# One attention stage of a fused two-layer model: values first, one tiled run per step, input normalised by GpSimd

## The reference

```python
q = (x @ Wq + bq).reshape(B, S, H, Dh).transpose(0, 2, 1, 3)   # x = layernorm(h), H = 12, Dh = 16
k = (x @ Wk + bk).reshape(B, S, H, Dh).transpose(0, 2, 1, 3)
v = (x @ Wv + bv).reshape(B, S, H, Dh).transpose(0, 2, 1, 3)
scores = jnp.einsum('bhqd,bhkd->bhqk', q, k) / SCALE
attn = jax.nn.softmax(scores, axis=-1)
out = jnp.einsum('bhqk,bhkd->bhqd', attn, v)
out = out.transpose(0, 2, 1, 3).reshape(B, S, D)
return out @ Wo + bo                                            # h = h + this
```

## Time and profile before

| what | us |
|---|---|
| median of three runs | 1070.24 (1067.24 to 1072.44) |
| the profiled execution | 1065.48 |
| its span | 1063.7 |
| PE busy | 801.3 (75%) |
| VectorE busy | 580.3 (55%) |
| ScalarE busy | 427.6 (40%) |
| GpSimd busy | 302.2 (28%) |

### The profile page before, as it was taken

The page is one execution under the profiler, slowest core; times in us unless marked ns, Lnnn a source line. Parts: engine busy times, 40 slices in busy tenths (PEclk is TensorE's granted clock), DMA queues, the critical chain, the costliest instruction groups (busy, mean ns, idle before and its releaser), DMA issues. The chain is left out here.

```text
span 1063.7 us, 22703 instructions
## 1 busy us (share of the span) xinstructions
PE 801.3 (75%) x7528; PEld 664.2 (62%) x7529; DVE 580.3 (55%) x1434; ACT 427.6 (40%) x1054; POOL 302.2 (28%) x293
## 2 busy tenths in 40 slices
PE   2489999998779814444455698895349999999993
PEld 2367777776679502222234476674249999999993
DVE  1757777776545101111116488886975666555562
ACT  4355666565543300000000267653524444444441
POOL 1300001000023000000000157761575555555552
PEclk7699999997555766666687699997558999999997
DMA  9391000000000398998960830002611333332331
GB/s 269 105 428 57 1 0 0 0 0 1 1 1 2 113 347 352 381 349 325 337 231 6 318 132 1 0 0 59 161 50 32 53 52 52 47 51 50 52 52 19
DMA packets 37999, 119.33 MB, mean 112 GB/s; under 512 B 7538, under 2 KB 28436, under 8 KB 33588
## 3 DMA queue, kind: packets, MB, share of 16 engines
q1 hardware_dynamic: 24980, 104.30, 26.9%
q0 software_dynamic: 10848, 12.67, 7.4%
q10 hardware_dynamic: 2112, 1.57, 0.9%
HBM read 105.77 MB, written 11.14 MB: 110 GB/s over the span
## 5 line engine op out<-in xcount | busy, mean ns | idle before, releaser
L1012 PE MATMUL psum<-flat,m_yT 64*32 64x384 f32 x624 | 45.8, 648 | 105.2 <-issue 103.9
L1629 POOL DMA_INDIRECT out_h<-x_ys,idx x55 | 87.5, 1591 | 98.9 <-ACT x_ys L1654 80.5
L1753 PE MATMUL psum<-w_pairs,x_h_hi 128*128 x330 | 101.7, 370 | 1.1 <-DVE x_h_lo L1681 1.1
L1012 PEld LDWEIGHTS psum<-flat,m_yT 64*32 64x32 f32 x624 | 16.9, 138 | 128.7 <-issue 128.4
L969 DVE COPY f_hid<-psum 128x384 f32<-128x384 f32 x16 | 8.9, 558 | 147.4 <-PE psum L1012 147.4
L1755 PE MATMUL psum<-w_pairs,x_h_lo 128*128 x330 | 82.7, 251 | 0.0
L1681 DVE TENSOR_TENSOR x_h_lo<-psum,x_h_hi 128x384 fp32r<-128x384 f32 x110 | 56.3, 553 | 38.7 <-ACT x_h_hi L1650 38.6
L1205 POOL MEMSET b_ones<- 96x96 f32 x1 | 0.2, 176 | 242.2 <-POOLq L130 242.2
L461 POOL TENSOR_TENSOR flat<-flat,a_bo 96x192 f32 (+1 forms) x32 | 18.7, 586 | 174.5 <-DVE a_xn L520 174.5
L534 DVE TENSOR_REDUCE a_mx<-psum 96x12 f32<-96x1152 f32 x32 | 43.3, 1353 | 44.0 <-PE psum L610 44.0
L1654 ACT ACTIVATE x_ys<-x_ys,cw 128x192 f32<-128x192 f32 x55 | 25.1, 456 | 102.0 <-DVE x_ys L1692 102.0
(11 more groups left out here) (271 smaller groups left out, 2293.8 us busy)
## 6 DMA issues: line engine op xcount, KB each, us to landing
flat<-in_slot_w SPq DMA_DIRECT2D x27, 2304.0 KB, 21.4
ring_last<-in_slot_w SPq DMA_DIRECT2D x5, 2304.0 KB, 28.9
flat<-in_moe_w SPq DMA_DIRECT2D x1, 10752.0 KB, 29.3
flat<-in_x_patches SPq DMA_DIRECT2D x4, 1536.0 KB, 16.2
out_h<-flat SPq DMA_DIRECT2D x1, 2304.0 KB, 12.2
xtab<-flat SPq DMA_DIRECT2D x4, 576.0 KB, 4.0
m_y<-in_fc_b SPq DMA_DIRECT2D x1, 1536.0 KB, 19.5
m_y<-f_y2g ACTq DMA_DIRECT2D x16, 96.0 KB
```

What stands on the lines that cost most here:

```text
L1012: mm = pe.matmul(b_h[n][r][B * c:B * (c + 1), :], g.yT[rows, k, SC * gr + c, :], w1[c // 2][rows, c % 2, k, n * N2:(n + 1) * N2], start=(k ...
L1629: pool.indirect_dma_start(out=A["out"][:, :], out_offset=bass.IndirectOffsetOnAxis(ap=g.idx[:, i:i + 1], axis=0), in_=ys[:, i % 2, :], in_ ...
L1753: pe.matmul(b_y[u % 2], h_hi[:, k, :], g.w_pairs[:, :, k, bass.ds(e, 1), :].rearrange("p two a d -> p two (a d)"), start=(k == 0), stop=False)
```

## The change

The edits, all within `attention0`:

- PE's order becomes values (lag 4, was 3; all three rounds in a row), scores, transpose of x, eight turns, output, q projection, last four turns, k and v projection.
- `project` is cut in two: q with its own semaphores, then k and v. The k part waits until ScalarE has copied q, since both lie in one PSUM bank, and the v part until x of the next batch has been copied out of bank 0.
- ScalarE's order becomes x copy, two copies of turned rounds, q copy, third copy, k copies, v copy, exponent (lag 2, was 3).
- VectorE's order becomes division, maximum, residual (lag 4, was 5), subtraction; the normalisation goes to GpSimd, ahead of the bias.

```diff
+            def norm_input(b, i):
+                reused(pool, s_xTp, b, 2)
+                pool.tensor_scalar(xn[:, i % 2, :].unsqueeze(1), g.h[:, bass.ds(b, 1), :], g.rstd[:, bass.ds(b, 1)],
+                                   g.nmr[:, bass.ds(b, 1)], ALU.mult, ALU.add).then_inc(s_xn, 1)
...
-            steps(pool, B, [(add_bias, 0)])
+            few_steps(B, [(norm_input, 0), (add_bias, 0)], UNROLL)
...
+            def q_copy(b, i):
+                item(act, s_qp, b)
                 reused(act, s_sc, b, 2)
-                act.activation(qT[:, i % 2, :, :], bank_qk[:, 0:2, :], ACT.Copy)
+                act.activation(qT[:, i % 2, :, :], bank_q[:, :, :], ACT.Copy).then_inc(s_qs, 1)
...
-            steps(act, B, [(exponent, 3), (qk_copy, 1), (v_copy, 1), (p_copy_first, 3), (x_copy, 0),
-                           (p_copy_last, 3)])
+            steps(act, B, [(x_copy, 0), (p_copy_first, 3), (q_copy, 1), (p_copy_last, 3), (k_copy, 1), (v_copy, 1),
+                           (exponent, 2)])
...
-            few_steps(B, [(divide, 4), (residual, 5), (norm_input, 0), (maximum, 2), (subtract, 2)], UNROLL)
+            few_steps(B, [(divide, 4), (maximum, 2), (residual, 4), (subtract, 2)], UNROLL)
...
+            def project_kv(b, i):
+                item(pe, s_qs, b)
+                for m in range(2, 4):
+                    mm = project(bank_k, i % 2, m)
+                mm.then_inc(s_kp, 1)
+
+                pe.wait_ge(s_xTs, min(b + 2, B) if isinstance(b, int) else b + 2)
...
+            def values(b, i):
                 item(pe, s_vs, b)
-
-                reused(pe, s_res, b, 2)
+                item(pe, s_pTs, b, NG)
+
+                reused(pe, s_res, b, 1)
                 reused(pe, s_oTs, b, 1)
-                values(b, i, 0)
-                turn(b, i, 2)
-                values(b, i, 1)
-                values(b, i, 2).then_inc(s_oTp, 1)
+                for r in range(NG):
...
-            steps(pe, B, [(project, 1), (turn_first, 3), (score, 2), (transpose_x, 0), (attend, 3), (output, 4)])
+            steps(pe, B, [(values, 4), (score, 2), (transpose_x, 0), (turn_first, 3), (output, 4), (project_q, 1), (turn_last, 3),
+                          (project_kv, 1)])
```

More of the change, by code:

```diff
@@ L429, in attention0 @@
         s_set, s_vset = sem("set"), sem("vset")
-        s_xn, s_bo, s_xTp, s_xTs, s_qkp, s_vp, s_qks, s_vs = (
-            sem(n) for n in ("xn", "bo", "xTp", "xTs", "qkp", "vp", "qks", "vs"))
+        s_xn, s_bo, s_xTp, s_xTs, s_qp, s_kp, s_vp, s_qs, s_ks, s_vs = (
+            sem(n) for n in ("xn", "bo", "xTp", "xTs", "qp", "kp", "vp", "qs", "ks", "vs"))
         s_sc, s_mx, s_sub, s_exp, s_sum = (sem(n) for n in ("sc", "mx", "sub", "exp", "sum"))
@@ L438, in attention0 @@
         bank_x = g.ps[:, 0, :]
-        bank_qk = g.ps[0:HALF, 1, 0:4 * T].rearrange("p (m t) -> p m t", t=T)
+        bank_q = g.ps[0:HALF, 1, 0:2 * T].rearrange("p (m t) -> p m t", t=T)
+        bank_k = g.ps[0:HALF, 1, 2 * T:4 * T].rearrange("p (m t) -> p m t", t=T)
         bank_oT = g.ps[:, 2, 0:NG * T].rearrange("p (r t) -> p r t", t=T)
@@ L478, in x_copy, with k_copy @@
                                bank_x[0:HALF, 0:2 * T].rearrange("p (k t) -> p k t", k=2), ACT.Copy).then_inc(s_xTs, 1)
-            def qk_copy(b, i):
-                item(act, s_qkp, b)
+            def q_copy(b, i):
+                item(act, s_qp, b)
                 reused(act, s_sc, b, 2)
-                act.activation(qT[:, i % 2, :, :], bank_qk[:, 0:2, :], ACT.Copy)
+                act.activation(qT[:, i % 2, :, :], bank_q[:, :, :], ACT.Copy).then_inc(s_qs, 1)
+            def k_copy(b, i):
+                item(act, s_kp, b)
+                reused(act, s_sc, b, 2)
                 for par in range(2):
-                    ins = act.activation(kT[:, i % 2, :, par, :], bank_qk[:, 2:4, :], ACT.Copy, scale=hmask[:, par:par + 1])
-                ins.then_inc(s_qks, 1)
+                    ins = act.activation(kT[:, i % 2, :, par, :], bank_k[:, :, :], ACT.Copy, scale=hmask[:, par:par + 1])
+                ins.then_inc(s_ks, 1)
             def v_copy(b, i):
@@ L496, in exponent, with p_copy @@
                 act.activation(p[:, i % 2, :, :], p[:, i % 2, :, :], ACT.Exp, scale=DH ** -0.5).then_inc(s_exp, 1)
[L498 to L503, removed]
+            def p_copy(b, r):
+                act.wait_ge(s_pTp, b * NG + r + 1)
+                reused(act, s_oTp, b, 1)
+                act.activation(pT[:, r, :, :], bank_pT[r].rearrange("p (h t) -> p h t", t=T), ACT.Copy).then_inc(s_pTs, 1)
             def p_copy_first(b, i):
-                p_copy(b, (0, 1))
+                p_copy(b, 0)
+                p_copy(b, 1)
             def p_copy_last(b, i):
-                p_copy(b, (2,))
-            steps(act, B, [(exponent, 3), (qk_copy, 1), (v_copy, 1), (p_copy_first, 3), (x_copy, 0),
-                           (p_copy_last, 3)])
+                p_copy(b, 2)
+            steps(act, B, [(x_copy, 0), (p_copy_first, 3), (q_copy, 1), (p_copy_last, 3), (k_copy, 1), (v_copy, 1),
+                           (exponent, 2)])
             layernorm_scale(None, act, g, s_ln)
@@ L516, in _ @@
         def _(v):
[L518 to L521, removed]
             def residual(b, i):
@@ L584, in transpose_x @@
                 item(pe, s_xn, b)
-                reused(pe, s_vs, b, 1)
+                reused(pe, s_vs, b, 2)
+                reused(pe, s_xTs, b, 1)
                 for hf in range(2):
@@ L589, in transpose_x, with project, project_q @@
                 mm.then_inc(s_xTp, 1)
-            def project(b, i):
-                item(pe, s_xTs, b)
-                reused(pe, s_qks, b, 1)
-                k = i % 2
[L595 to L600, removed]
+            def project(bank, xk, m):
+                pe.matmul(bank[:, m % 2, :], wqk[0:HALF, 0, m * HALF:(m + 1) * HALF], xT[0:HALF, xk, 0, :],
+                          start=True, stop=False)
+                return pe.matmul(bank[:, m % 2, :], wqk[:, 1, m * HALF:(m + 1) * HALF], xT[:, xk, 1, :],
+                                 start=False, stop=True)
+            def project_q(b, i):
+                item(pe, s_xTs, b)
+                reused(pe, s_ks, b, 1)
+                for m in range(2):
+                    mm = project(bank_q, i % 2, m)
+                mm.then_inc(s_qp, 1)
+            def project_kv(b, i):
[4 more added lines that the diff above has]
+                pe.wait_ge(s_xTs, min(b + 2, B) if isinstance(b, int) else b + 2)
+                k = i % 2
                 pe.matmul(bank_x[0:T, 2 * T:2 * T + D], xT[0:HALF, k, 0, :], wv[0:HALF, 0, :], start=True, stop=False)
@@ L604, in score @@
             def score(b, i):
-                item(pe, s_qks, b)
+                item(pe, s_ks, b)
                 reused(pe, s_sub, b, 1)
@@ L618, in turn @@
                 mm.then_inc(s_pTp, 1)
[L620 to L625, removed]
             def turn_first(b, i):
@@ L631, in turn_first, with turn_last @@
                 turn(b, i, 1)
-            def attend(b, i):
+            def turn_last(b, i):
+                pe.wait_ge(s_pTs, b * NG + 1)
+                turn(b, i, 2)
+            def values(b, i):
                 item(pe, s_vs, b)
-                reused(pe, s_res, b, 2)
+                item(pe, s_pTs, b, NG)
+                reused(pe, s_res, b, 1)
                 reused(pe, s_oTs, b, 1)
-                values(b, i, 0)
-                turn(b, i, 2)
-                values(b, i, 1)
-                values(b, i, 2).then_inc(s_oTp, 1)
+                for r in range(NG):
+                    for j in range(HG):
+                        mm = pe.matmul(bank_oT[HPAD * j:HPAD * (j + 1), r, :], vv[:, i, head_at(r, j), :], pT[:, r, j, :],
+                                       start=True, stop=True, tile_position=(0, HPAD * j))
+                mm.then_inc(s_oTp, 1)
             def output(b, i):
```

## The result

The changed kernel takes 1052.36 us (median of four runs, 1051.24 to 1054.57) against 1069.05 for the kernel before (four runs, 1067.24 to 1072.44). The ratio is 0.985, its 95% interval 0.981 to 0.989: faster by 1.5%. The forecast was 1046.4 and the range 1036 to 1062. The direction and the mechanism in the steps held; the gain, 16.7 us, is 0.7 of the 23.8 forecast, and the parts are further off than the sum. The kernel before ran again beside the experiments, in three groups with medians of 1067.87, 1065.80 and 1067.67 us; against those the gain is 13.4 to 15.5. The profiled execution took 1051.24 (span 1049.3); there the stage, from the first slot product on PE to the last statistics, fell from 221.0 to 207.7 us.

What follows compares the result with a forecast made beforehand. PE was taken to set the pace: 28 steps shortened by 0.68 us give 19.0, fill 1.5 and drain 3.3, together 23.8 us off the 1070.24 median: 1046.4 us, range 1036 to 1062.

Steps and rivals of the forecast that it cites:

- PE sets the pace of the steps: First attention's 28 steps: PE's order alone takes each from 6.35 to 5.67 us, 19.0 us in all.
- The normalisation's move: Normalisation on GpSimd instead of VectorE: 0.6 us taken there, fits in the step, costs nothing; VectorE's 0.3 is off the path.
- The new wait for the q copy: PE at the k projection: release 0.58 us after the q projection, less four turns of 0.34, a 0.24 wait per step.
- PE work of 5.43: PE per step: pieces of 5.01 us plus three boundaries of 0.14; bounds 5.3 to 5.85.
- The three boundaries: PE switching between full-size and tiled matmuls: v to values, values to scores, scores to x; 0.14 us each.
- The walk of the other engines: VectorE, ScalarE and GpSimd through a 5.67 us step: nothing else binds; slack 0.0 at output, 0.1 at eight turns.
- rival 1: Steps: the walk's thin slacks are missing, the ring runs 0.3 late, step 5.97, 15.4 us gained, 1055; chance 10%.
- rival 2: Steps: GpSimd's doubled work collides with VectorE's division, step about 6.22, 8.4 us gained, 1062; chance 6%.
- Fill, -1.5 forecast: Start of the stage: scores come earlier but values a step later; 1.5 us gained, bounds 0 and 3.
- half clock within the steps: Sign that the forecast is wrong: PE at half clock inside steps, where full clock to the last step was expected.
- Rival 4: PE's clock falls in the steps, each costing 3.7 us more; 1098 with half of them; chance 8%.
- Drain, -3.3 forecast: End of the stage: 21.6 us against 24.9, last turns at half clock; 3.3 gained, bounds 0 and 5.

Runs made afterwards that it cites:

- the two moves of the q projection: On the changed kernel, PE's q projection moved ahead of the output product: 1046.15 us; moved behind the last four turns instead: 1061.8 us.
- the filler runs: Changed kernel plus unused full-size PE products at waits before the first full step: 1047.35 us alone, 1045.89 us with unused products ahead of the stage too.
- idle work ahead: 60 bf16 and 6 fp32 unused PE products added ahead of the stage: 1050.0 us on the changed kernel, 1063.75 us on the kernel before.
- both filler and idle work: Changed kernel plus unused PE products ahead of the stage and unused full-size ones at waits before the first full step: 1045.89 us.
- all in one: Changed kernel plus early q projection, subtraction ahead of the residual, and unused PE products ahead of the stage and in the fill: 1033.32 us.

## Why the prediction was right, and where it was not

- **PE sets the pace of the steps, and its order alone shortens them**: right. 5.80 to 5.88 against 5.67, in the bounds. The normalisation's move was costed at nothing, and undoing it changed nothing (5.80 and 1052.27 us).
- **The new wait for the q copy**: right in place and size. The forecast was 0.58 less four turns of 0.34, 0.24 on PE. In the rows, turns and wait take 0.58, and the two moves of the q projection changed the step by -0.26 and +0.34.
- **PE work of 5.43**: 0.13 to 0.15 too low. The three boundaries were about right: values 0.63 for 0.51 of streaming, scores 0.18 over, v 0.10 over. What I left out is the restart: the first k product after the wait costs 0.07 more, the output product's first 0.06, and the loop a further 0.02 on average. The range of 5.3 to 5.85 for PE's work with 0.24 on top held it. "TensorEngine Tiling (Array Packing)", Key Properties, in the Trainium skill says that a change of tiling mode drains TensorE; the trace agrees in that each of these boundaries costs time, 0.10 to 0.18 us here, but it does not show that a drain is the reason.
- **The walk of the other engines**: right. The exponent starts straight behind the v copy (162.06), VectorE waits 1.16 for the values, and the output product has no wait in the list. Its slack is the 0.0 of the forecast: VectorE's result is there at 163.99 and the product starts at 164.06. Neither rival 1 nor rival 2 came, the second by a narrow miss: VectorE's multiplication ends at 163.58, 0.09 before GpSimd starts at 163.67, where I had 0.1. GpSimd's work met a two-input instruction of VectorE in no profile of this stage, so that rule remains untested here.
- **Fill, -1.5 forecast, +4.4 measured, and 3.1 more in the first full steps**: this step failed. I carried the clock of the earlier trace rows over: in the one profile I had, the kernel before was at full clock from 56.0 us. The changed order stayed at half clock until 77.8 to 82.5 us in all seven profiles without filler (its own, and those of the variants), and "half clock within the steps", one of my own signs of being wrong, came true in the first full steps. That the clock is the price, and not the new waits, is shown by the filler runs: with the clock up throughout, the fill takes 16.6 us, where the forecast was 18.3 less 1.5. Rival 4 had the right mechanism in the wrong place: I looked for it in the steps and not in the fill.
- **Why the clock rose so late** is not shown. The changed order cuts the first projection, 16 products of q and k and four of v in one piece before, by the wait for q, and it would be easy to call this the cause. But in the second profile of the kernel before the same uncut piece ran from 50.85 to 55 us and the clock stayed at half until 67.6; with idle work ahead it fell at 53.0 and rose at 76.9. So part of the +4.4 is that the profile of before which I compare with had an early rise; against the second one it is 0.5.
- **Drain, -3.3 forecast, -6.0 measured**: the steps of latency went as forecast, but I priced the last turns at half clock, and in this profile the clock held to 255.6 us (the turns at 249.90 take 0.86). In four variants it fell at 233 to 243 us, and from the last scores to the end they took 15.1 to 15.3 us instead of 12.5. One of them, with both filler and idle work, has the changed order itself and a drain of 21.7, where the forecast was 21.6. So the larger gain is luck of the execution.
- **The bounds and chances**: 1038 to 1058 does not follow from the terms beside it; added up they give 1037 to 1066 (fill and drain 3.2 less or 4.8 more). Rival 2 has 6% in the list and 5 in the sum of the chances.

The 10.5 us missing in the stage are thus 4.2 of step and 9.0 at the start, less 2.7 at the end, and the last statistics came at 256.35 instead of near 247. With the drain that I forecast the total would have been about 1055, still in the range; the last 2.7 us towards the forecast are luck. The medians differ by 16.7 us and the profiled executions by 14.2. The kernel before has executions of up to 1078 us, at a mean clock of 0.82 where most have 0.83; none of these was profiled, and the late start that was (1063.93 us) was not slow, so what makes them long is open.

## What to carry to other kernels

A wait for a copy out of a shared PSUM bank is priced from rows before it exists: copy, release and the modelled tail, less what stands between; then put enough between. In a software pipeline, look at the fill and the drain apart from the steady step: they run other mixes of work, and the fill can stay at half clock for 25 us while the step behind it is as fast as planned. One profile shows one start: take a second one of the kernel before, and compare the fills, before giving a clock to a changed order or blaming the order for it.

## What was not expected of the hardware

- PE can be busy 9.59 of 10 us and 5.00 of 5 us in its row and stay at 1.2 GHz; with unused full-size products among the same work, and nothing added ahead, 2.4 GHz came at 55.9 us instead of 78.1, when two of the 15 had run, and stayed. All three versions with these products were at full clock by then, none of the seven changed orders without them before 77.8. The kernel before, with no filler, reached it at 56.0 us in one execution and at 67.6 in another. "TensorE: Matmul & The Clock Gate", Part 4, in the Trainium skill says that a PE-mode transpose does not count as busy in the same way; these runs do not separate transposes from tiled products.
- A full clock was lost at 49.0 us (idle work ahead, changed kernel) and at 49.1 (all in one), 1.0 and 1.3 us after the second block of added products had begun; PE had been idle for 3.24 and 3.00 us ahead of that block. Where that idle time was 2.50 us (idle work and filler) the clock stayed up.
- GpSimd normalises 96 x 192 values with two per-partition operands in 0.50 us, less than its two-input addition of the same size (0.59).
